# A four-layer graph and FFN kernel: the second FFN set prepared alone and first, x added by VectorE, and the last 17 sort columns weighed and moved one by one

## What is computed

```python
edge_index = jnp.stack([src, dst])
x = x + _L0_gnn_ref(_layernorm(x), edge_index, W, a_l, a_r)      # graph attention, 4 heads
x = x + _L0_ffn_ref(_layernorm(x)[None], ..., wr, br, w1, b1, w2, b2)[0]
x = x + _L1_gnn_ref(_layernorm(x), src, dst, edge_type, self_W, self_b, rel_W)
x = x + _L1_ffn_ref(_layernorm(x)[None], router_w, w1, b1, w2, b2)[0]   # 8 experts, top 2

# _L0_ffn_ref, n = layernorm(x), 3125 tokens:
weights = n @ wr + br                       # one score for each token
_, idx = top_k(weights, 1562); sel = the first 1561 of idx
y = (gelu(n @ w1 + b1) @ w2 + b2) * weights      # of the chosen tokens alone
out = n + y
```

## Time and profile before

| | |
|---|---|
| median of 3 runs | 1909.75 us (1907.54 to 1911.23) |
| profiled execution | 1906.33 us |
| its span | 1904.4 us |
| PE, DVE, ACT, POOL busy | 1430.0, 1225.3, 606.2, 1329.3 us |
| first sort's last step to the first gather | 219.03 to 231.18 us |
| FFN on PE, first up to last down | 831.75 to about 1033.5 us |
| relation table on PE | about 1034.4 to 1125.5 us |

### The profile page before, as it was taken

How to read it: one execution, slowest core, us unless ns; L and a number is a source line. 1 busy time by engine, 2 the same in 40 slices (tenths; PEclk the granted TensorE clock), 3 DMA queues, 4 the chain that set the end, 5 groups by cost and what they waited for, 6 DMA issues and landing times.

```text
span 1904.4 us, 23016 instructions
## 1 busy us (share of the span) xinstructions
PE 1430.0 (75%) x6382; PEld 967.0 (51%) x6382; DVE 1225.3 (64%) x2866; ACT 606.2 (32%) x1753; POOL 1329.3 (70%) x1335
## 2 busy tenths in 40 slices
PE   5566567778888887767999977666666667786993
PEld 3233246556555555545886434434433333375992
DVE  6999977788988987747334115454444444477655
ACT  0687411136666664132323320000000000015435
POOL 0688577777777777779886727777777777723666
PEclk9799778989999999888999988898876777656996
DMA  4011143445644444310201565333333333314556
GB/s 96 10 32 32 18 106 106 107 105 134 146 117 120 119 116 106 107 26 1 66 1 24 142 178 172 106 105 106 106 105 105 105 105 105 106 36 134 155 155 186
DMA packets 110952, 186.05 MB, mean 98 GB/s; under 512 B 31578, under 2 KB 78125, under 8 KB 110701
## 3 DMA queue, kind: packets, MB, share of 16 engines
q0 software_dynamic: 56480, 134.84, 27.6%
q1 hardware_dynamic: 54349, 49.75, 9.3%
HBM read 152.80 MB, written 31.43 MB: 97 GB/s over the span
## 4 chain that ended last, share of the span: by engine, by line
POOL 35%; PE 27%; DVE 17%; issue 13%; DMA 7%; DVEq 0%; ACT 0%; POOLq 0%; SPq 0%; ACTq 0%
POOL gath L934 32%; DVE hot_c L675 6%; PE ps L980 5%; DMA gath<-y_tab,index_b 5%; PE ps L1455 5%; PE ps L1419 4%; PE ps L1404 3%; PE ps L1893 3%; PE ps L1904 3%; DVE hot_r L666 2%; POOL slot_tab_b L762 1%; DMA gath<-h_tab,index_a 1%; DVE acc L970 1%; DVE junk_d L1312 1%; PE ps L1629 1%
## 5 line engine op out<-in xcount | busy, mean ns | idle before, releaser
L980 PE MATMUL ps<-gath,hot 128*125 128x260 f32 (+1 forms) x1808 | 598.7, 471 | 289.9 <-DVE gath L1019 96.9
L980 PEld LDWEIGHTS ps<-gath,hot 128*125 128x125 f32 x1808 | 365.3, 222 | 482.5 <-DMA gath<-y_tab,index_b 193.6
L934 POOL DMA_INDIRECT gath<-h_tab,index_a x464 | 446.9, 963 | 149.6 <-issue 138.3
L934 POOL DMA_INDIRECT gath<-y_tab,index_b x440 | 416.1, 946 | 166.8 <-issue 119.7
L970 DVE TENSOR_TENSOR acc<-acc,ps 125x257 f32 (+1 forms) x672 | 284.6, 424 | 317.8 <-PE ps L980 279.3
L707 PE MATMUL ps<-hot_c,pay 125*128 125x440 f16 (+1 forms) x901 | 195.4, 370 | 63.4 <-ACT pay L696 59.3
L762 POOL DMA_INDIRECT slot_tab_b<-sent_word_b,sent_to_b x136 | 167.3, 1230 | 36.3 <-issue 36.3
L752 POOL DMA_INDIRECT slot_tab<-sent_word,sent_to x102 | 130.2, 1277 | 81.6 <-DVE sent_to L514 50.8
L696 ACT ACTIVATE pay<-hot_r,plan_b 125x128 f16<-125x128 f16 x578 | 172.0, 386 | 0.0
L707 PEld LDWEIGHTS ps<-hot_c,pay 125*128 125x128 f16 x901 | 87.9, 101 | 162.7 <-ACT pay L696 80.8
L1019 DVE TENSOR_TENSOR gath<-gath,ps 128x1024 f32<-128x1024 f32 x116 | 136.0, 1214 | 0.0
(11 more groups left out here) (360 smaller groups left out, 1980.0 us busy)
## 6 DMA issues: line engine op xcount, KB each, us to landing
y_tab<-ybuf SPq DMA_DIRECT2D x25, 448.0 KB
y_slots<-y_buf SPq DMA_DIRECT2D x64, 128.0 KB
gath<-h_tab,index_a POOLq DMA_INDIRECT x464, 2.8
gath<-y_tab,index_b POOLq DMA_INDIRECT x440, 2.8
h_tab<-hbuf SPq DMA_DIRECT2D x25, 113.8 KB
xa<-in_x SPq DMA_DIRECT2D x1, 2800.0 KB
xa<-in_x SPq DMA_DIRECT2D x5, 560.0 KB
xn_tab<-acc SPq DMA_DIRECT2D x5, 560.0 KB
```

The source lines that it names most:

```text
L934: p.indirect_dma_start(gath[:, ring(k) + s, 0:width], None, table, bass.IndirectOffsetOnAxis(ap=index[g][:, col:col + 1], axis=0)).then_in ...
L980: ins = t.matmul(sum_p(g, q, width), hot[:, s, :], gath[:, s, 0:width], start=(e == 0), stop=(e == n - 1))
```

## The change

In the first sort's 19th step ACT signals after every column and PE waits for every column. `left_scores` is split: the maximum stays where it was, the five instructions that make the parts move behind the 19th step. In the FFN, DVE adds x for sets 1 to 4 itself; set 1 is divided, added, measured and normed alone and first, and sets 2 to 4 follow together. ACT has a root more (set 1 behind chunk 1 of the first up, sets 2 to 4 ahead of tile 3's turn copy), SEND_FIRST is 8, and the places of the choice's matmuls move. Later numbers of `norm_ready` and `var_ready` grow by one, and `first_root` has eight cells.

```diff
-SEND_FIRST, SEND_NORMED, SEND_FFN = 16, 1, 3
+SEND_FIRST, SEND_NORMED, SEND_FFN = 8, 1, 3
-CHOICE_AT = ((1, "up", 2), (1, "up", 6), (2, "up", 1), (2, "up", 4), (2, "up", 7), (2, "down", 1), (2, "down", 3), (3, "up", 2))
+CHOICE_AT = ((1, "down", 0), (1, "down", 1), (2, "up", 1), (2, "up", 4), (2, "up", 7), (2, "down", 1), (2, "down", 3), (2, "down", 4))
...
+    one_by_one = lambda g, i: g == "a" and i == A_STEPS - 1
...                                                      # weigh_step
-        ins.then_inc(weighed[g], 1)
+            if one_by_one(g, i):
+                ins.then_inc(weighed[g], 1)
+        if not one_by_one(g, i):
+            ins.then_inc(weighed[g], 1)
...                                                      # move_step
-        t.wait_ge(weighed[g], 2 * i + c + 1)
+        if not one_by_one(g, i):
+            t.wait_ge(weighed[g], 2 * i + c + 1)
         for j in range(*CHUNKS[c]):
+            if one_by_one(g, i):
+                t.wait_ge(weighed[g], 2 * i + j + 1)
...                                                      # front_vector
             if i == A_STEPS - 2:
-                left_scores(v)
+                right_maximum(v)
+        left_scores(v)
         unpack_words(v)
...                                                      # ffn_pool
-        p.wait_ge(x_in, STORE * (1 + SETS))
-        for i in range(1, SETS):
-            p.wait_ge(acc_normed, i + 1)
-            p.tensor_tensor(xa[:, set_of(i), :], xa[:, set_of(i), :], acc3[:, set_of(i), 0:D], ALU.add).then_inc(x1_made, 1)
...                                                      # ffn_vector
-        inverse(v, rest)
-        for i in range(1, SETS):
-            divided(v, set_of(i)).then_inc(acc_normed, 1)
-        for i in range(1, SETS):
-            v.wait_ge(x1_made, i)
-            measure(range(i * U5, (i + 1) * U5))
-        v.wait_ge(vector_step, vn.n)
-        norm_sums(v, rest)
-        norm_scale(v, 3, rest)
+        inverse(v, set_of(1, SETS - 1))
+        divided(v, set_of(1)).then_inc(acc_normed, 1)
+        add_x(1)
+        v.wait_ge(x1_made, 1)
+        measure(range(U5, 2 * U5))
+        v.wait_ge(vector_step, vn.n)
+        norm_sums(v, set_of(1))
+        divided(v, set_of(2)).then_inc(acc_normed, 1)
+        norm_scale(v, 3, set_of(1))
         v.wait_ge(norm_ready, 3)
         for t in range(U5, 2 * U5):
             norm(t)
         v.wait_ge(ffn_in, FFN_IN)
-        for t in range(NT):
-            if t + 2 * U5 < NT:
-                norm(t + 2 * U5)
+        for t in range(U5):
+            dot(t)
+        for i in range(3, SETS):
+            divided(v, set_of(i)).then_inc(acc_normed, 1)
+        for i in range(2, SETS):
+            add_x(i)
+        for i in range(2, SETS):
+            v.wait_ge(x1_made, i)
+            measure(range(i * U5, (i + 1) * U5))
+        v.wait_ge(vector_step, vn.n)
+        norm_sums(v, rest)                               # rest is now sets 2 to 4
+        for t in range(U5, 2 * U5):
+            dot(t)
+        norm_scale(v, 4, rest)
+        v.wait_ge(norm_ready, 4)
+        for t in range(2 * U5, NT):
+            norm(t)
             dot(t)
...                                                      # ffn_scalar
-                if i == 0 and c == 5:
-                    norm_root(a, 3, set_of(1, SETS - 1))
+                if i == 0 and c == 1:
+                    norm_root(a, 3, set_of(1))
             for t in range(i * U5, (i + 1) * U5):
+                if t == 3:
+                    norm_root(a, 4, set_of(2, SETS - 2))
```

More of the change, by code:

```diff
@@ L165, in build @@
     stats = base.tile("stats", [NP, NT, 6])
-    first_root, first_exp = (base.tile(n, [1, 1]) for n in ("first_root", "first_exp"))
+    first_root, first_exp = base.tile("first_root", [1, 8]), base.tile("first_exp", [1, 1])
     mean, var, tmp25, rstd, nmr = (base.tile(n, [NP, NT]) for n in ("mean", "var", "tmp25", "rstd", "nmr"))
@@ L578, in norm_root @@
     def norm_root(a, n, at):
-        a.activation(first_root[:, :], ones[0:1, 0:1], ACT.Sqrt)
+        a.activation(first_root[:, n:n + 1], ones[0:1, 0:1], ACT.Sqrt)
         a.wait_ge(var_ready, n)
@@ L785, in words_sync, with right_maximum @@
         s.dma_start(hi_s[:, :], rows).then_inc(words_back, 16)
+    def right_maximum(v):
+        v.wait_ge(h_copied, NT)
+        v.tensor_reduce(gm[:, :], hrl[:, :, 0:HEADS].rearrange("p t h -> p h t"), AX, ALU.max).then_inc(gm_ready, 1)
     def left_scores(v):
@@ L790, in left_scores @@
         hl = hrl[0:NP, :, HEADS:]
-        v.wait_ge(h_copied, NT)
         v.tensor_copy(parts[:, :, :, 0], hl).then_inc(vector_step, vn.up())
@@ L1300, in ffn_vector @@
     def ffn_vector(v):
-        rest = set_of(1, SETS - 1)
+        rest = set_of(2, SETS - 2)
         def measure(tiles):
@@ L1313, in dot, with add_x, norm @@
                                    accum_out=w_dot[:, t:t + 1]).then_inc(dotted, 1)
-        v.wait_ge(added["a"], PAIRS)
-        inverse(v, rest)
-        for i in range(1, SETS):
+        def add_x(i):
+            v.wait_ge(acc_normed, i + 1)
+            v.tensor_tensor(xa[:, set_of(i), :], xa[:, set_of(i), :], acc3[:, set_of(i), 0:D], ALU.add).then_inc(x1_made, 1)
+        def norm(t):
+            v.tensor_scalar(acc_cols(t, D), flat(xa, t), rstd[:, t:t + 1], nmr[:, t:t + 1], ALU.mult, ALU.add).then_inc(x_normed, 1)
+        v.wait_ge(added["a"], PAIRS)
+        inverse(v, set_of(1, SETS - 1))
[7 more added lines that the diff above has]
+        norm_scale(v, 3, set_of(1))
+        v.wait_ge(norm_ready, 3)
+        for t in range(U5, 2 * U5):
+            norm(t)
+        v.wait_ge(ffn_in, FFN_IN)
+        for t in range(U5):
+            dot(t)
+        for i in range(3, SETS):
             divided(v, set_of(i)).then_inc(acc_normed, 1)
-        for i in range(1, SETS):
+        for i in range(2, SETS):
+            add_x(i)
+        for i in range(2, SETS):
             v.wait_ge(x1_made, i)
@@ L1323, in ffn_vector @@
         norm_sums(v, rest)
-        norm_scale(v, 3, rest)
-        v.wait_ge(norm_ready, 3)
-        def norm(t):
-            v.tensor_scalar(acc_cols(t, D), flat(xa, t), rstd[:, t:t + 1], nmr[:, t:t + 1], ALU.mult, ALU.add).then_inc(x_normed, 1)
         for t in range(U5, 2 * U5):
+            dot(t)
+        norm_scale(v, 4, rest)
+        v.wait_ge(norm_ready, 4)
+        for t in range(2 * U5, NT):
             norm(t)
-        v.wait_ge(ffn_in, FFN_IN)
-        for t in range(NT):
-            if t + 2 * U5 < NT:
-                norm(t + 2 * U5)
             dot(t)
@@ L1344, in ffn_vector @@
                 norm_sums(v, set_of(0, SETS - 1))
-                norm_scale(v, 4, set_of(0, SETS - 1))
-                v.wait_ge(norm_ready, 4)
+                norm_scale(v, 5, set_of(0, SETS - 1))
+                v.wait_ge(norm_ready, 5)
                 for t in range(U5):
@@ L1360, in ffn_vector @@
         norm_sums(v, set_of(SETS - 1))
-        norm_scale(v, 5, set_of(SETS - 1))
-        v.wait_ge(norm_ready, 5)
+        norm_scale(v, 6, set_of(SETS - 1))
+        v.wait_ge(norm_ready, 6)
     def ffn_scalar(a):
-        a.activation(first_root[:, :], ones[0:1, 0:1], ACT.Gelu_apprx_tanh)
+        a.activation(first_root[:, 0:1], ones[0:1, 0:1], ACT.Gelu_apprx_tanh)
         a.wait_ge(ffn_in, FFN_IN)
@@ L1435, in table_pool @@
     def table_pool(p):
-        p.wait_ge(norm_ready, 5)
+        p.wait_ge(norm_ready, 6)
         p.memset(acc[:, :], 0.0).then_inc(pool_ready, 1)
@@ L1461, in table_scalar @@
             if step == 2:
-                norm_root(a, 5, set_of(SETS - 1))
+                norm_root(a, 6, set_of(SETS - 1))
             t = step
@@ L1540, in relation_scalar @@
     def relation_scalar(a):
-        a.wait_ge(norm_ready, 5)
+        a.wait_ge(norm_ready, 6)
         for i in range(NT):
@@ L1550, in relation_scalar @@
         a.copy(r_t[:, :, :], ps[:, 0, 0:2 * EXP].rearrange("p (k e) -> p k e", k=2)).then_inc(rt_copied, 1)
-        a.activation(first_root[:, :], ones[0:1, 0:1], ACT.Sqrt)
+        a.activation(first_root[:, 0:1], ones[0:1, 0:1], ACT.Sqrt)
     def relation_tensor(t):
@@ L1610, in route_scalar @@
         a.activation(prob[:, :, :], logit[:, :, :], ACT.Exp).then_inc(prob_exp, 1)
-        a.activation(first_root[:, :], ones[0:1, 0:1], ACT.Gelu)
+        a.activation(first_root[:, 0:1], ones[0:1, 0:1], ACT.Gelu)
     def route_tensor(t_eng):
@@ L1684, in route_vector @@
             if k == 0:
-                norm_scale(v, 6, every)
+                norm_scale(v, 7, every)
             v.wait_ge(vector_step, vn.n)
```

7 lines of the change are left out of this document (3 added, 4 removed).

## The result

The changed kernel takes 1882.11 us (median of 4 runs, 1881.52 to 1883.41) where the kernel before takes 1909.07 beside it: a ratio of 0.9854 (95% interval 0.9842 to 0.9866), 27.0 us less. The forecast was 1887.0, 22.8 less. The direction, the places and the order of the engines in the chain came out as written; the gain was 4 us larger, so that the time lies at the very low end of the range, and one term of the sum, POOL's bound in the FFN, was too small.

What follows compares the result with a forecast made beforehand. The bound changes by stage: DVE's row in the first sort, PE's stall in the FFN, then POOL's chain. Gains of 2.0 + 20.8 = 22.8 us from 1909.75 gave 1887, range 1882 to 1894.

Steps and rivals of the forecast that it cites:

- POOL's bound: FFN: POOL's chain from tile 10 to tile 19's b2 addition limits the gain to 20.8 us (18.0 plus 2.8 slack).
- The sort: End of the first sort: unpacking starts 2.0 us earlier, with bounds of 1.4 and 3.1 us.
- DVE's row: First sort: DVE's last one-hot ends at 225.44, the parts at 226.80, then unpacking instead of at 228.82: 2.0 us.
- PE's side of the FFN: FFN: PE gains 24.2 us if nobody else is late; between 22.5 and 24.2 with DVE's lateness.
- three terms: PE in the FFN: 20.1 us idle, 2.6 for the slow first down tile, 1.5 waiting for the choice's votes.
- The upper bound of 1 us for ACT's root: FFN, ACT's root behind chunk 1 of the first up: PE's wait for a gelu taken as 0, at most 1 us.
- What DVE loses beside POOL: FFN, sets 2 to 4: POOL's tile additions cost DVE's two divisions and three additions 2.6 us.
- the higher estimate: FFN, by the skill's blocking rule: each of DVE's five operations could wait up to 0.73 us, 3.7 in all.
- The first one: FFN: PE is the bound to the end, FFN gains 24.2, whole 26.2, time 1883.5; chance 0.2.
- The second: FFN: DVE slowed more beside POOL, tile 10 at 872, total gain 17.5, time 1892; chance 0.2.
- The third: Stage behind the FFN: POOL's words return late; 1897 with 10 us given back; chance 0.03.
- The fourth: FFN: without its pause PE's clock falls, 2.6 us more per down tile, eleven make the kernel slower; chance 0.02.

Runs made afterwards that it cites:

- two_at_end_c: Changed kernel with two words instead of three sent beside the last five of POOL's 20 b2 additions; 1878.5 us against 1907.98 for the kernel before, ratio 0.9844.
- first_16: Changed kernel with 16 words instead of 8 sent ahead of the FFN; 1892.51 us, 11.1 more than the changed kernel.
- pool_later: Changed kernel, but POOL's sixth addition to x waits for DVE's scale of sets 2 to 4; 1891.39 us, 9.95 more than the changed kernel.
- after_again: Changed kernel, unchanged, run again on a chip like the first; 1881.44 us against 1907.43 for the kernel before, ratio 0.9866.
- split_only: Kernel before with only the parts of left_scores moved behind step 19, last chunk still in two pieces; ratio 0.9995 to the kernel before.
- sort_only_c: Kernel before with only both edits of the first sort, on a chip like the first; ratio 0.9983 to the kernel before.
- pool_adds: Changed kernel, but POOL makes the four additions to x, set 1 first; 1900.75 us, ratio 0.9968, 19.3 more than the changed kernel.

## Why the prediction was right in kind, and the step that failed

**The sort: right.** 2.0 us were foreseen, by DVE's row; 2.1 measured. PE ends within the 1.36 us of the parts, as worked out.

**PE's side of the FFN, 24.2: right,** and it is PE's floor (178.4 against the 177.9 of `two_at_end_c`). Each of its three terms is in the rows: no wait of 20.1, the first down tile in 3.62 us, no wait at the choice. The upper bound of 1 us for ACT's root beside the gelus wasn't used on a chip like the first; on the slower ones PE waits there for 0.30 to 1.08 us in five of the seven profiles with the new FFN.

**POOL's bound, 20.8: right in kind, 2.8 too small,** and this is the step that failed. The FFN gained 23.5 us in the first profile of the changed kernel and 24.1 in the second. The sum put the b2 addition of tile 19 at 1005.3 on the time axis of before; it was at 999.46 + 2.99 = 1002.45, where 2.99 is the distance between the two first ups (831.75 and 828.76). Of these 2.8 us, 2.1 lie in DVE's way to tile 10: POOL's addition of it was put at 867.8 and stood at 865.7. The first norm came at 840.0 on that axis instead of 840.7, the two divisions and three additions took 8.6 us (843.39 to 851.99) instead of 9.7, and the measuring, the sums and the scale were shorter by some tenths. Another 1.0 is POOL's own pace: 14 additions with their words took 893.04 - 862.70 = 30.34 us, 2.17 each, where I had 2.24, a mean over a stretch of before in which eight of the words took 1.37 to 1.41 us instead of 1.20. Against it, the b2 additions up to tile 19 took 99.8 us, 0.3 more than counted. With 23.6 for POOL in place of 20.8, the sum would have been 25.6 and the forecast 1884. The runs show that the mechanism is the one named: `first_16` and `pool_later` delay POOL alone, and PE waits for all of the delay.

**What DVE loses beside POOL.** I had 2.6 us on the five operations, and 3.7 as the higher estimate. `first_16` has them with POOL silent, `after_again` with POOL beside them, rows of DVE in this order:

```profile
842.12 2.89 DVE L1115 TENSOR_TENSOR acc<-acc,dinv 125x1280 f32<-125x1280 f32 x2
844.93 4.29 DVE L1325 TENSOR_TENSOR xa<-xa,acc 125x1280 f32<-125x1280 f32 x3
```

```profile
842.54 3.43 DVE L1115 TENSOR_TENSOR acc<-acc,dinv 125x1280 f32<-125x1280 f32 x2
845.89 4.82 DVE L1325 TENSOR_TENSOR xa<-xa,acc 125x1280 f32<-125x1280 f32 x3
```

Added up, 7.2 alone and 8.2 beside POOL (8.7 in the first profile), so 1.1 to 1.6 us. In `pool_later`, where POOL is silent from 850 on, the five dots behind them take 2.5 us instead of 3.7. The larger share of the contention fell on POOL, whose words beside them took up to 2.25 us where they take 1.20 alone, and POOL had time there: it still waited for DVE at tile 10.

**The rivals.** The first one, PE as the bound to the end, was nearly the case (0.8 us from it in one profile, 0.4 in the other), and for the reason given beside it: tile 10 came earlier and POOL's steps were shorter. 0.2 was too little for a case that needed 3.4 us out of a sum of many terms, nearly all of which I had taken on the careful side. The second (DVE slowed more) pointed the wrong way. The third didn't happen: the last word was sent by 1083.1, and the words were back at 1101.1, behind the same load as before. The fourth, a lower clock without the pause, didn't either: the granted clock was 1.00 from 828.8 to 1007. Where the traces show a lower clock in the FFN, PE had stood idle before: 0.57 behind 20.10 us, 0.54 behind 9.67, 0.76 behind 11.86.

**The rest.** 22.8 forecast, plus 2.8 for POOL's chain, plus 0.1 for the sort is 25.7; measured were 27.0 and 26.0. The remaining 0.3 to 1.3 us is no more than the stages outside the change differ between two profiles of the same kernel (2.0 us in the expert stage); what it is made of is not shown.

## What to carry to other kernels

When a stall goes, work out the next bound from rows with the same neighbours: the pace of POOL and the contention of DVE were taken from stretches with other work beside them, and nearly all errors pointed the same way. When several terms are taken on the careful side, add up what they come to together, and give the case behind them the chance that this sum deserves. And look for a date of need in every queue that an operation stands in, not only in that of its consumer: set 1's root was due at ACT 8 us before PE wanted the tile.

## What the runs showed of the hardware

- Waiting can cost twice. Behind an idle time of 9.67 us PE's clock was 0.54 and a tile took 6.64 instead of 3.62 us. In the old FFN, the 32 matmuls behind the choice's wait took 8.66 us after a wait of 2.15 (`split_only`), and 10.35 after one of 2.79 (`sort_only_c`), at these clocks, again the last column but two:

```profile
896.40:905.00 8.60, 8.60 (x35) 6.17 (x35) 0.61 (x4) 3.70 (x7) 7.72 (x9) 1.00 0.05 1
```

```profile
896.10:906.40 10.30, 10.30 (x35) 7.19 (x35) 0.61 (x4) 3.71 (x7) 9.21 (x10) 0.83 0.06 1
```

- In `pool_adds` an operation of 125x5 elements on DVE took 2.85 us instead of the 0.17 of `after_again`, with POOL's addition of 125x1280 (2.88 us) begun 0.05 us earlier. The Trainium skill (SBUF — State Buffer, "Who interferes with whom") says that the ports shared by the two engines are an exclusive lock, and that the order of issue decides who is blocked; here the trace agrees. Beside POOL's short additions (0.73 us) DVE's norms of set 1 took 0.60 us instead of 0.34, and its dots 0.75 and, behind tile 10, up to 0.93 instead of 0.42. On a slower chip, where four divisions of DVE and four additions of POOL ran side by side in the kernel before, they took 11.10 and 15.07 us; 5.70 and 11.38 are the times without this.
- POOL's words, each a DMA, took 2.23 to 2.25 us beside DVE's divisions and additions, and 1.20 alone. The same section of the Trainium skill infers that such operations of DVE don't hold up the making of descriptors; in this trace something does, and whether it is these operations was not tried.
- POOL stands still for 7.1 to 7.7 us between its last word and its first addition to x, in the six profiles of the changed kernel and its variants on chips like the first. Later, where words and additions take turns, there is no such pause (0.02 to 0.23 us between them); what it is, is open.
- Chips run the same program 14% apart, 272 us in two profiles of the kernel before. Of these 212 lie in three stages that are paced by gathers (587.0 and 689.5 us, 548.8 and 637.7, 100.1 and 121.0), while a gather lasts 946 and 949 ns and PE's first up 17.00 us on both. A stall between two engines can be 20 us on one and 6 on the other.
